# Two-layer transformer kernel: part of the last block's opening laid beside the last group of cross heads

## What is computed

```python
x = _layernorm(x + _L1_attn_ref(x, w_qkv, w_out))            # 16 heads of 16, causal
x = _layernorm(x + _L1_xattn_ref(x, ctx, ctx, mask, Wq, bq, Wk, bk, Wv, bv, Wo, bo))  # 16 heads, 1601 keys
x = _layernorm(x + _L1_ffn_ref(x, ...))
# _L1_ffn_ref: residual + 0.5 * (silu(LN(x) @ w1 + fc1_bias) @ w2 + fc2_bias)
# w1 (256x1024), w2 (1024x256): (q - 128) * scales
```

## Time and profile before

| | us |
|---|---|
| median of 3 runs | 2063.3 (2062.9 to 2066.65) |
| profiled execution, its own time | 2063.18 |
| span in the profile | 2061.1 |
| TensorE busy | 1811.4 (88%) |
| VectorE busy | 1428.5 (69%) |
| ScalarE busy | 1063.8 (52%) |
| GpSimd busy | 710.5 (34%) |
| mean granted TensorE clock | 0.936 |

### The profile page before, as it was taken

How to read it: one execution, slowest core, us unless ns; L and a number is a source line. 1 busy time by engine, 2 the same in 40 slices (tenths; PEclk the granted TensorE clock), 3 DMA queues, 4 the chain that set the end, 5 groups by cost and what they waited for, 6 DMA issues and landing times. The chain is left out here.

```text
span 2061.1 us, 32786 instructions
## 1 busy us (share of the span) xinstructions
PE 1811.4 (88%) x12562; PEld 1031.0 (50%) x12562; DVE 1428.5 (69%) x2391; ACT 1063.8 (52%) x1706; POOL 710.5 (34%) x786
## 2 busy tenths in 40 slices
PE   8888888893999999947999989869999999998687
PEld 4677655672888888833333365512222222221455
DVE  1432368774677777767778558889999999991644
ACT  1111144450656555523666723318888888787242
POOL 0574286501344444423233014321541212100543
PEclk9999999995999999977899999959999999998789
DMA  5014087756466666534111037611311101000101
GB/s 183 19 62 135 35 296 249 257 205 251 180 258 263 259 249 239 184 115 131 25 32 34 9 132 212 198 37 58 95 47 24 34 17 34 17 17 1 51 1 41
DMA packets 107743, 241.62 MB, mean 117 GB/s; under 512 B 28362, under 2 KB 79086, under 8 KB 103600
## 3 DMA queue, kind: packets, MB, share of 16 engines
q1 hardware_dynamic: 80484, 199.43, 27.5%
q0 software_dynamic: 24992, 38.00, 6.6%
q10 hardware_dynamic: 2112, 2.10, 0.3%
HBM read 182.09 MB, written 56.79 MB: 116 GB/s over the span
## 5 line engine op out<-in xcount | busy, mean ns | idle before, releaser
L1772 DVE TENSOR_REDUCE Eh_maxima<-Eh_max 128x2 f32<-128x802 f32 x512 | 474.7, 987 | 22.9 <-PE Eh_max L1657 16.0
L1760 ACT ACTIVATE Eh_probs<-Eh_pair 128x1024 f32<-128x1024 f32 (+1 forms) x288 | 287.8, 999 | 117.0 <-PE Eh_pair L1696 117.0
L1152 PE MATMUL C_y<-C_x_high,C_W 128*128 128x256 f16 x1472 | 250.2, 274 | 1.5 <-DVE C_x_low L1389 1.5
L1657 PE MATMUL Eh_max<-Eh_KS,Eh_QS 49*128 49x401 f16 x1024 | 198.4, 358 | 51.9 <-DVE Eh_maxima L1772 41.7
L1719 PE MATMUL Eh_av_ps<-Eh_probs,E_V 128*17 128x512 f32 (+1 forms) x1664 | 226.0, 616 | 0.0
L1152 PE MATMUL C_y<-C_x_low,C_W 128*128 128x256 f16 x736 | 201.5, 274 | 0.0
L1772 DVE TENSOR_REDUCE Dh_maxima<-Dh_max 128x2 f32<-128x1024 f32 x128 | 152.1, 1221 | 46.7 <-PE Dh_max L1665 42.7
L1760 ACT ACTIVATE Eh_probs<-Eh_single 128x512 f32<-128x512 f32 x272 | 161.5, 594 | 21.3 <-PE Eh_single L1696 21.2
L1657 PEld LDWEIGHTS Eh_max<-Eh_KS,Eh_QS 49*128 49x128 f16 x1024 | 50.5, 94 | 240.8 <-DVE Eh_maxima L1772 201.3
L1500 POOL DMA_DIRECT2D Eh_KS<-E_kd x64 | 37.2, 582 | 356.5 <-PE Eh_pair L1696 350.7
L1152 PEld LDWEIGHTS C_y<-C_x_high,C_W 128*128 128x128 f16 x1472 | 144.6, 98 | 18.9 <-issue 1.9
(11 more groups left out here) (367 smaller groups left out, 3702.2 us busy)
## 6 DMA issues: line engine op xcount, KB each, us to landing
C_W<-w_split SPq DMA_DIRECT2D x23, 3072.0 KB, 11.1
w_split<-B_w_parts SPq DMA_DIRECT2D x24, 768.0 KB, 4.6
B_places<-in_w_experts_dram SPq DMA_DIRECT2D x18, 768.0 KB, 6.0
Eh_KS<-E_kd POOLq DMA_DIRECT2D x64, 150.1 KB, 3.3
C_tail<-in_expert_tail_dram SPq DMA_DIRECT2D x23, 384.0 KB, 8.0
A_QT<-in_w_experts_dram SPq DMA_DIRECT2D x8, 768.0 KB, 5.2
w_split<-A_QT SPq DMA_DIRECT2D x8, 768.0 KB, 6.8
early_ctxT<-in_ctxT_dram SPq DMA_DIRECT2D x6, 800.5 KB, 5.8
```

The source lines that it names most:

```text
L1152: last = mm(y_ps[n % Y_BANKS][:, i, :], W[:, u, a, at_w:at_w + P], x[:, s % 2, k, :], start=(q == 0), stop=(q == len(parts) - 1))
L1657: last = self.nc.tensor.matmul(bank[:, a, 0:self.cw], self.QS[r, slot, p, qt * P:(qt + 1) * P], self.KS[r, slot, p, k0:k0 + self.cw], star ...
L1760: self.nc.scalar.activation(dst, src, ACT.Exp, scale=1.0 / SCORE).then_inc(self.exp_done, 1)
L1772: self.nc.vector.tensor_reduce(self.maxima[:, g % 2, :, p * TPB + qt, c], self.max_ps[n % 2][:, :, 0:self.cw], AX_X, ALU.max).then_inc(sel ...
```

## The change

- The block of cross heads gets a helper, `LastStart`. It holds the output projection, the two norms and the turned input of the feed-forward, in SBUF that stays for the last block. Its items run inside the last group: one after the third score and after every second one from there. They do the bias product, the output projection and first norm of batches 0 to 2, second norm of batches 0 and 1, and the turned input of batch 0. They use the banks `max_ps`, which the last group doesn't need but for two tokens. VectorE, not ScalarE, copies the turned halves and scales HT there.
- Before the token of group 14, TensorE waits until the items' banks are read.
- The split first matrix stays in SBUF; the order of the two is swapped, so that only the second is stored and loaded again.
- VectorE's wait for all stores at the start of the heads is gone. In the cross heads SP waits for them, then loads the helper's weights.
- No clearing of semaphores between cross heads and last block; no drain of GpSimd at the end of heads.
- In the last block, turn of batch 1 comes first, then the first 8 widens; the attended turn of batch 3 stands behind four of them, its projection behind widen (1, 1) and a narrow, the turns of batches 2 and 3 behind steps (1, 5) and (2, 5). GpSimd makes their low parts behind the low parts of steps 14 and 22.
- Self phase: normalization of batch 0 before `mix(1, 0)`; loads of the constants behind those of Y.

```diff
@@ Heads.walk
         for step in range(GROUPS):
+            between = iter(range(len(START_ITEMS)) if self.start is not None and step == GROUPS - 1 else ())
+            scores = 0
             for kind in self.order:
+                if kind == "T":
+                    for i in between:
+                        yield "X", i
...
                 elif kind in "SB":
                     yield "S", s
-                    s += 1
+                    s, scores = s + 1, scores + 1
+                    if scores >= START_AFTER and (scores - START_AFTER) % 2 == 0:
+                        for i in between:
+                            yield "X", i
+                            break
@@ Heads.tensor
+            if kind == "X":
+                if k == 0:
+                    pe.wait_ge(self.read, n)
+                self.start.tensor(pe, START_ITEMS[k])
             if kind == "T":
+                if k == GROUPS - 2 and self.start is not None:
+                    self.start.banks_free(pe)
                 self.turn_token(pe, n, k)
@@ Heads.vector
-        self.places.all_stored(dve)
...
+            if kind == "X":
+                self.start.vector(dve, START_ITEMS[k])
@@
+START_ITEMS = (("shift",), ("attended", 0, 0), ("attended", 0, 1), ("attended", 1, 0), ("project", 0), ("attended", 1, 1), ("project", 1),
+               ("attended", 2, 0), ("project", 2), ("attended", 2, 1), ("project", 3), ("project", 4), ("project", 5), ("turn", 0), ("turn", 1))
+START_AFTER = 3
@@ LastStart
+    def banks_free(self, pe):
+        pe.wait_ge(self.after.sum_ready, (B - 1) * TPB // 2)
+        pe.wait_ge(self.copied, KD)
...
+    def vector(self, dve, item):
...
+        if kind == "attended":
+            c, h = at
+            dve.wait_ge(after.turned, KD * c + h + 1)
+            v.tensor_copy(self.XT[:, h, c * S:(c + 1) * S], after.turn_ps[h]).then_inc(after.copied, 1)
+        if kind == "project":
+            j = at[0]
+            after.add_pair(dve, j)
+            if j == 1:
+                after.norm.statistics(dve, 0, after.sum_ready, per=2)
+            if j == 2:
+                self.again(dve, 0)
+            if j == 3:
+                after.norm.statistics(dve, 1, after.sum_ready, per=2)
+            if j == 4:
+                self.normed_again(dve, 0)
+            if j == 5:
+                self.again(dve, 1)
+                after.norm.statistics(dve, 2, after.sum_ready, per=2)
+        if kind == "turn":
+            h = at[0]
+            dve.wait_ge(self.turned, h + 1)
+            v.tensor_scalar(self.HT[:, 0, h, :], after.turn_ps[h], self.gamma[:, h:h + 1], self.beta[:, h:h + 1], ALU.mult, ALU.add).then_inc(self.copied, 1)
+            if h == KD - 1:
+                dve.wait_ge(self.copied, KD)
+                v.tensor_copy(self.HT_parts[:, 0, 0], self.HT[:, 0]).then_inc(self.ht_high, 1)
+                self.normed_again(dve, 1)
...
+    def pool(self, pool):
+        after, norm_in = self.after, self.norm_in
+        after.norm.setup(pool)
+        norm_in.setup(pool)
+        for c in range(B - 1):
+            after.base(pool, c)
+        after.norm.inverse_deviation(pool, 0)
+        norm_in.inverse_deviation(pool, 0)
+        after.norm.inverse_deviation(pool, 1)
+        after.base(pool, B - 1)
+        norm_in.inverse_deviation(pool, 1)
+        after.norm.inverse_deviation(pool, 2)
+        self.low(pool, 0)
+        pool.wait_ge(self.weights.stored, 16)
@@ run_heads
-    with nc.Block() as block:
+    with nc.Block(no_gpsimd_drain=True) as block:
...
+            if heads.start is not None:
+                heads.places.all_stored(sp)
+                heads.start.sync(sp)
@@ phase_self
-                mix(1, 0)
                 norm.normalize(dve, 0)
+                mix(1, 0)
@@ phase_last, TensorE
             turn(1)
-            pe.wait_ge(w_loaded, 32)
...
+            for j in range(NF // 2):
+                widen(0, j)
+            pe.wait_ge(copied, 2 * KD)
+            after.attended(pe, B - 1)
             for j in range(NF // 2, NF):
                 widen(0, j)
+            pe.wait_ge(w_loaded, 16)
             for c in range(1, B):
                 for j in range(NF):
                     widen(c, j)
                     narrow(c - 1, j // 2, range(NF // 2) if j % 2 == 0 else range(NF // 2, NF))
+                    if (c, j) == (1, 1):
+                        after.project(pe, B - 1)
+                    if (c, j) == (1, 5):
+                        turn(2)
+                    if (c, j) == (2, 5):
+                        turn(3)
@@ phase_last, ScalarE
+            act.wait_ge(small_loaded, 32)
             turn(1)
+            for n in range(B * NF):
                 step(n)
+                if n == NF // 2 - 1:
+                    copy_turned(nc, act, XT, turn_ps, B - 1, after.turned, after.copied)
+                if n == NF + 5:
+                    turn(2)
...
@@ phase_last, GpSimd
+            norm_out.setup(pool)
+            start.low(pool, 1)
+            low(0)
             norm_in.inverse_deviation(pool, 2)
+            for n in range(1, B * NF):
+                low(n)
...
+                if n in (NF + 6, 2 * NF + 6):
+                    start.low(pool, n // NF + 1)
@@ phase_last, VectorE
+            step(0)
+            start.again(dve, 2)
+            step(1)
+            step(2)
             dve.wait_ge(half_b2, 1)
             base(0)
+            for j in range(3, NF):
+                step(j)
...
@@ build_program
-            renew_semaphores(nc)
```

More of the change, by code:

```diff
@@ L1505, with __init__ @@
 class Heads:
-    def __init__(self, ctx, nc, name, n_keys, places, V, ATT, idents, tri, ahead, behind, order):
-        self.nc, self.n_keys, self.causal = nc, n_keys, places.causal
+    def __init__(self, ctx, nc, name, n_keys, places, V, ATT, idents, tri, ahead, behind, order, start=None):
+        self.nc, self.n_keys, self.causal, self.start = nc, n_keys, places.causal, start
         self.places, self.KS, self.QS, self.slots, self.R = places, places.KS, places.QS, places.slots, places.R
@@ L1836, in __init__, with make_banks @@
             self.need = 48
+    def make_banks(self, ctx):
+        self.turn_ps = [ctx.enter_context(self.nc.psum_tensor(f"{self.name}_turn{i}", [P, S], F32)) for i in range(KD)]
+        self.out_ps = [ctx.enter_context(self.nc.psum_tensor(f"{self.name}_out{i}", [P, 2, D], F32)) for i in range(2)]
     def sync(self, sp):
@@ L1956, in split @@
         g.tensor_tensor(self.parts[:, 1, :], self.w, self.parts[:, 0, :], ALU.subtract).then_inc(self.low, 1)
-        pool.wait_ge(self.low, i + 1)
-        pool.dma_start(self.dst[i], self.parts[:]).then_inc(self.stored, 16)
+        if i == 0:
+            pool.wait_ge(self.low, 1)
+            pool.dma_start(self.dst, self.parts[:]).then_inc(self.stored, 16)
     def beside(self, pool, g):
@@ L1987, in _ @@
                     beside.beside(pool, g)
+            if heads.start is not None:
+                heads.start.pool(pool)
         @block.tensor
@@ L2240, in phase_cross1 @@
         after = OutProjection(own, nc, "Do", X, XT, ATT, ident, dram["self_WoT"], None)
+        after.make_banks(own)
         v_ps = after.out_ps
@@ L2522, in turn @@
             def turn(c):
-                pe.wait_ge(norm_in.normed, (c + 1) * TPB)
-                pe.wait_ge(after.copied, KD * B)
-                if c >= 1:
-                    pe.wait_ge(copied, KD * c)
                 for h in range(KD):
-                    for t in range(TPB):
-                        last = nc.tensor.transpose(turn_ps[h][:, t * P:(t + 1) * P], normed_tile(c * TPB + t)[:, h * P:(h + 1) * P], ident[:])
-                    last.then_inc(turned, 1)
+                    start.turn_half(pe, c, h)
             def widen(c, j):
@@ L2675, in _ @@
             v = nc.vector
-            def again(c):
-                after.norm.normalize(dve, c)
-                norm_in.statistics(dve, c, after.norm.normed)
-            def normed_again(c):
-                dve.wait_ge(norm_in.rstd_ready, c + 1)
-                dve.wait_ge(after.turned, KD * (c + 1))
-                for t in range(c * TPB, (c + 1) * TPB):
-                    v.tensor_scalar(normed_tile(t), X[:, t, :], norm_in.mv[:, t, 0:1], norm_in.rstd[:, t:t + 1],
-                                    ALU.subtract, ALU.mult).then_inc(norm_in.normed, 1)
             def base(c):
@@ L2740, in _ @@
                     step(c * NF + j)
+                    if (c, j) == (1, 0):
+                        start.normed_again(dve, 2)
+                    if (c, j) == (1, 1):
+                        after.add(dve, 3)
+                        after.norm.statistics(dve, 3, after.sum_ready, per=2)
+                        dve.wait_ge(base_ready, 1)
+                    if (c, j) == (1, 3):
+                        base(1)
+                    if (c, j) == (1, 4):
+                        start.again(dve, 3)
+                    if (c, j) == (2, 0):
+                        start.normed_again(dve, 3)
```

(13 more changed lines are left out.)

285 lines of the change are left out of this document (133 added, 152 removed).

## The result

The changed kernel took 2053.64 us in the median of 12 runs (2043.99 to 2069.65), the kernel before 2064.43 beside it (12 runs, 2055.91 to 2068.57): a ratio of 0.9949, 95% interval 0.9924 to 0.9974, 10.8 us less. Two later comparisons of the same pair (e1, e12) gave 0.9916 (0.9901 to 0.9931) and 0.9931 (0.9908 to 0.9953). The mean of the three is 0.9932, or 14 us. The prediction was 2037, range 2026 to 2049. The median of 2053.64 lies above that range: the sign came as forecast, but of the 26.5 us that were forecast the first comparison has 10.8, and the mean of the three has 14, 12.5 too few.

A forecast was written before the change was run, and what follows sets the result against it. VectorE bounds the cross heads before their last group, TensorE the last block's dense part; the last group has little TensorE room. Terms -4.2 - 1.0 - 0.9 + 11.6 - 32 = -26.5 us from 2063.18 give 2037, range 2026 to 2049.

The forecast's parts named there:

- Step 3: Boundary between cross heads and last block: no clearing of semaphores, no GpSimd drain; -0.9 us, bounded by 0 and -1.5.
- signs of being wrong: Forecast wrong if the last group grows under 7 or over 17 us, or the last block takes under 113 or over 127.
- Step 1: Start of self and cross heads: VectorE no longer waits for the last stores before the first maximum; -4.2 us for both.
- Step 2: Self phase: normalization of batch 0 ahead of batch 1's first mix, constants loaded behind the Y tiles; -1.0 us.
- Step 4: Last group of cross heads: 15 items added on TensorE lengthen it from 37.2 to 48.8 us, +11.6 (bounds +6.4, +20).
- Step 5: Last block's opening: first widen of batch 1 at 23 us instead of 66.0, -43 us.
- Step 6: Last block's dense part, with two 3.4 us TensorE stalls and an unchanged last 21.4 us; block 120 against 152.2 us, -32.
- A: Rival: the last group hides the moved work, clock full, VectorE on time, only +5 to 7 us; 2031, chance 0.17.
- B: Rival: a VectorE and GpSimd chain bounds the last group or opening, +13 us; 2050 at most, 2045 typical, chance 0.2.
- C: Rival: last block's gaps at widen of batches 2 and 3 are absent, GpSimd being early; -7 us, 2030, chance 0.05.
- D: Rival: slower than before, TensorE at 1.2 GHz through the whole last group, +45 us there; 2070, chance 0.03.
- E: Rival: the starts of the heads bring nothing, +4 us, within the forecast's range; no chance of its own given.

The follow-up runs named there:

- e1: The changed kernel unaltered, profiled a second time beside the kernel before; ratio 0.9916 (0.9901 to 0.9931).
- e12: The changed kernel unaltered, run once more beside the kernel before; ratio 0.9931 (0.9908 to 0.9953).
- e2: Changed kernel with the drain of GpSimd put back at the end of the self heads alone; ratio to the kernel before 0.9913, median 2041.14 us.
- e3: Changed kernel with the drain of GpSimd put back at the end of both kinds of heads; ratio to the kernel before 0.9922, median 2045.21 us.
- e9: Changed kernel with GpSimd's drain back at the self heads' end, plus a drain instruction in the cross heads where GpSimd is idle; ratio to the kernel before 0.9895.
- e4: Kernel before, with GpSimd's drain taken out at the end of both kinds of heads; ratio to the kernel before 1.0051, median +13.3 us.
- e6: Changed kernel with VectorE's wait for the last stores put back ahead of the first maximum in both heads; ratio to the kernel before 0.9958, median 2056.13 us.
- e11: Changed kernel with GpSimd's base of batch 3 moved from the last cross group to the last block's beginning; ratio to the kernel before 0.9945.
- e7: Changed kernel with ScalarE's wait for the small loads behind its scaling and cast of batch 1; ratio to the kernel before 0.9915.
- e5: Changed kernel with GpSimd's low parts of the input of batches 2 and 3 two hidden tiles earlier; ratio to the kernel before 0.9893.

## Why the prediction came out wrong

**Step 3 failed.** It said "no drain of GpSimd at the end of heads" and counted it as something removed, in the -0.9 of the boundary behind the cross heads. That boundary did shrink by 1.0 (0.5 against the 1.5 of the earlier trace rows). But the option doesn't remove the drain's price, it takes away the place where it was free. In before GpSimd had no work left for over 50 us when each kind of heads ended, and the drain hid beside them. In after the price comes up at the next place that waits for GpSimd: the barrier behind the self heads (+3.9 us, a boundary that step 3 never looked at, though the edit stands in the function that both kinds of heads run), and the end of the kernel (+4.7 us). e2 gives back the first alone, e3 and e9 both, and e4 brings the price into the kernel before. Together they are 8.6 of the 12.5 us between the forecast of -26.5 and the mean of 14. The prediction's own signs of being wrong could not catch this: the last group grew by 10.7 and the last block took 126.3 us, both inside their limits, and no sign looked at the boundary behind the self heads.

**Step 1** held in the self heads: the idle time of 2.10 us is down to 0.17, the stretch is 2.3 us shorter, and e6 brings 2.4 back. In the cross heads the idle time of 2.13 us is gone and e6 brings 1.91 back, but not the phase's length: that half of the -4.2 is not shown. Its reason, that VectorE runs without a gap behind the first maximum, was a misreading: in before VectorE waits 16.0 us there for TensorE's maximum products. **Step 2**: the normalization of batch 0 now starts behind the inverse deviation without the mix between them, as said; no run undid it by itself.

**Step 4**, +11.6, was +10.7 in the profile of after and in most others (56.2 against 45.5), +12.4 and +13.8 in e1 and e12. In after its size came out by luck, by two errors that nearly cancel. The clock was 1.00 through the whole group, so the 3.5 us for it weren't paid; and the rest of the group was some 2.6 us longer than summed. How these 2.6 divide isn't shown. One piece is TensorE's last token, which waits 2.65 us for a chain (normalization of 3.20 us, division, ScalarE's copy) that the sum had at 1.7. The estimate of "1.4 to 2.9 us" for such four tiles was short at its upper end, and e11 shows why for batch 0. In e1 and e12 the mean clock over the same stretch was 0.96 and 0.94, and the group took 1.7 and 3.1 us more than in after: there the clock's term was paid in part and nearly in full.

**Step 5** said 23 us, and it was 23.8. The wait for the small loads ended 4.4 us after the block's first work (4.7 said), and the table load stood on the path as said, 0.02 us behind the cast. Waiting for these loads ahead of the scaling costs 2.8 us, which e7 takes away; the prediction counted the wait, but didn't see that the scaling needs none of the loads. ScalarE: Activation LUTs of the Trainium skill (What ACT_TABLE_LOAD costs) adds a drain of about 1.4 us to a switch of tables; the trace shows none, for the load begins 0.02 us behind the cast, ends at 1939.35, and the first sigmoid begins at 1939.37.

**Step 6** said 120 us for the block and it was 126.3. Of the 6.3, 4.7 are the drain at its end, so the step "the last 21.4 us stay" failed, by step 3's error. The rest is 0.8 in the opening and some 0.8 in the dense part, within the scatter of these stretches: the two stalls measured 3.3 us each (3.4 said), put down to GpSimd as said, 25 us apart and not 21, and the low clock behind the second cost 1.9 us in place of 1 (six widen and twelve narrow products took 2.23 us each in the chain, in place of 1.29 and 1.31).

**The rivals.** A came only in its first half: the clock was full in after, but the group grew by 10.7 and not by 5 to 7. B's time, "2050 at most", is nearest to what came, but not by its mechanism: TensorE's waits from 1876 to 1927 name no VectorE at all, and the group grew by about the forecast's own term. C didn't come (e5 shows what it would have given), nor did D (the group's clock was 0.94 or more in every profile). E fell for the self heads by e6; for the cross heads it stays open. None of the rivals was a cost that moves to a place outside the edited stretch.

**What stays open.** Of the 12.5 us, 8.6 are the drains, some 1.6 the block. The last 2 us are within what three comparisons can tell, and two things could fill them: the half of step 1 in the cross heads (2.1 us), and the self heads, which carry 5 us more of low clock in five of the twelve profiles of changed kernels and in neither of the two of before. That may be chance; whether the change makes it more frequent was not tried. Step 2 and the removed clearing of semaphores were not undone by themselves either.

## What to carry to other kernels

When an edit drops a drain or a barrier, ask what it waited for and who will wait for it now: look at every later barrier up to the kernel's end, and for each engine at the idle stretch that used to cover it. Here a drain of the engine that had issued 165 transfers took over 9 us; put it by hand where that engine is idle. And where a function is shared by two phases, cost the edit in both.

## What the runs showed of the hardware that wasn't expected

- A drain on GpSimd took 9.3 to 9.5 us after the cross heads' transfers (165 in after's list), also in e3, where the last of them had been issued some 100 us before; behind the self heads it cost 3.9 us on the path. Paid once, it isn't paid again (a wait of 0.2 us at the end of e3 and e9).
- Four tiles normalized by VectorE from SBUF to SBUF take 1.37 us alone and 3.2 to 3.4 beside 2.2 to 2.4 us of GpSimd's work in SBUF; statistics of four tiles take 1.40 in both cases.
- At the start of the self heads the granted clock stays at its 1.2 GHz level for 34 us after the first maximum in one profile and for 48 in another of the same kernel, with TensorE nearly all busy between 990 and 1010 us; the self maxima are 5 us longer for it.
